# Zero matmuls ahead of the weights, the first x tile ahead of the score weights, the output weights in slot 25

## The reference, cut to what matters

```python
keys_flat = k @ Wk + bk                 # k: 32 x 512, the same for each batch
values = (keys_flat @ Wv + bv).reshape(B, S, H, D)
scores = jnp.einsum('blhe,bshe->bhls', (query @ Wq + bq).reshape(B, L, H, E), keys)
A = sparsemax(scale * scores)           # per row and head, over the 32 patterns
out = jnp.einsum('bhls,bshd->blhd', A, values)
out = jnp.transpose(out, (0, 2, 1, 3)).reshape(B, L, H * D) @ Wo + bo
x = layernorm(x + out)
s = jnp.einsum('btd,dm->btm', x, Win) + bin_
g = jnp.einsum('btmh,mh->btm', relu(s[..., None] * W1 + b1), W2) + b2
x = layernorm(x + g @ Wout + bout)
```

## Time and profile before

| | us |
|---|---|
| median of 3 runs | 1354.32 (1354.13 to 1356.15) |
| the profiled execution | 1352.76 |
| its span in the trace | 1351.0 |
| PE busy | 1251.9 (93%) |
| DVE busy | 1138.9 (84%) |
| ACT busy | 1053.6 (78%) |
| POOL busy | 703.2 (52%) |

### The profile page before, as it was taken

How to read it: one execution, slowest core, us unless ns; L and a number is a source line. 1 busy time by engine, 2 the same in 40 slices (tenths; PEclk the granted TensorE clock), 3 DMA queues, 4 the chain that set the end, 5 groups by cost and what they waited for, 6 DMA issues and landing times. The chain is left out here.

```text
span 1351.0 us, 25359 instructions
## 1 busy us (share of the span) xinstructions
PE 1251.9 (93%) x5838; PEld 867.3 (64%) x5838; DVE 1138.9 (84%) x4573; ACT 1053.6 (78%) x2269; POOL 703.2 (52%) x1674
## 2 busy tenths in 40 slices
PE   7982889999999999999999999999999999899962
PEld 6651666766776776776776776776776777555541
DVE  3977788889999999999999999999998999876764
ACT  2671756688898888899898898888899899666654
POOL 1330333345565555555556555555555556567663
PEclk9995999999999999999999999999999999999975
DMA  6380786555655655655655655655655655668733
GB/s 189 93 210 26 193 231 208 179 171 182 215 189 197 219 192 191 219 193 191 218 192 193 218 192 192 219 196 189 217 195 190 217 196 182 210 231 296 251 94 70
DMA packets 92374, 258.36 MB, mean 191 GB/s; under 512 B 16259, under 2 KB 16259, under 8 KB 75814
## 3 DMA queue, kind: packets, MB, share of 16 engines
q1 hardware_dynamic: 92198, 256.52, 58.7%
HBM read 206.13 MB, written 50.33 MB: 190 GB/s over the span
## 5 line engine op out<-in xcount | busy, mean ns | idle before, releaser
L663 PE MATMUL bank<-G_sb,pT 128*128 128x512 f32 x1024 | 461.1, 593 | 1.9 <-ACT pT L758 1.8
L663 PEld LDWEIGHTS bank<-G_sb,pT 128*128 128x128 f32 x1024 | 185.0, 191 | 185.9 <-issue 183.4
L1077 DVE MAX8 top<-bank 128x8 f32<-128x32 f32 x2048 | 212.3, 179 | 44.5 <-issue 44.5
L466 POOL TENSOR_TENSOR shift_sq<-sum,per_row_sq 128x1 f32<-128x1 f32 x256 | 96.0, 375 | 265.7 <-DVE y_sb L954 263.2
L771 ACT ACTIVATE unread<-y_sb,shift_sq 128x512 bf16<-128x512 f32 x256 | 183.9, 718 | 51.8 <-POOL minus_mean L468 51.7
L1115 DVE SCALAR_TENSOR_TENSOR acc<-hinge,w2c,acc 128x512 f32<-128x512 f32 x224 | 167.4, 748 | 61.7 <-ACT hinge L783 58.3
L783 ACT ACTIVATE hinge<-s_sb,b1c,w1c 128x512 f32<-128x512 f32 x256 | 205.8, 807 | 0.2
L588 PE MATMUL bank<-A_hi,xT_hi 128*128 128x512 f32 x512 | 204.0, 399 | 0.0
L590 PE MATMUL bank<-A_hi,xT_lo 128*128 128x512 f32 x512 | 203.9, 398 | 0.0
L589 PE MATMUL bank<-A_lo,xT_hi 128*128 128x512 f32 x512 | 203.7, 398 | 0.0
L481 POOL TENSOR_TENSOR rstd<-ve,minus_half 128x1 f32<-128x1 f32 x256 | 164.8, 644 | 43.1 <-POOL ve L476 42.8
(11 more groups left out here) (133 smaller groups left out, 2421.9 us busy)
## 6 DMA issues: line engine op xcount, KB each, us to landing
G_sb<-G_of_heads SPq DMA_DIRECT2D x128, 1024.0 KB, 5.4
x_sb<-in_L_attn_query_dram SPq DMA_DIRECT2D x128, 256.0 KB, 4.7
y_sb<-in_L_attn_query_dram SPq DMA_DIRECT2D x256, 128.0 KB, 5.4
out_dram<-o_sb SPq DMA_DIRECT2D x256, 128.0 KB, 4.7
G_of_heads<-y_sb SPq DMA_DIRECT2D x64, 256.0 KB, 3.8
y_sb<-in_L_attn_Wk_dram SPq DMA_DIRECT2D x1, 1024.0 KB, 5.7
y_sb<-in_L_attn_Wq_dram SPq DMA_DIRECT2D x1, 1024.0 KB, 8.2
y_sb<-in_L_attn_Wv_dram SPq DMA_DIRECT2D x1, 1024.0 KB
```

The costliest lines, as they stand in the source:

```text
L466: nc.gpsimd.tensor_tensor(shift_sq[:, par:par + 1], total[:, par:par + 1], per_row_sq[:], ALU.mult).then_inc(s_mean, 1)
L663: mm = nc.tensor.matmul(o_ps[i % 2][:], pT[:, bass.ds(pair_place(turn, i) + (i % H * C + c) * P, P)], G_sb[:, i % GR, c, :], start=(c == 0 ...
L1077: mx = nc.vector.max(top8[:, h, :], z_ps[i % 2][:, h * S:(h + 1) * S])
```

## The change

It does three things, and edits the waits that they need.

1. POOL fills `K_blk` (buffer `acc`) with zeros as its second fill instead of its fifth, and PE, once that fill is done, runs 7 float32 products of 128 x 128 by 128 x 256 on it into bank 7, before it waits for the keys' loads.
2. PE transposes x of tile 0 between "c" and "A" instead of after "A". ACT rounds it ahead of the first `A_hi`, DVE takes its rest ahead of the first `A_lo`. The scores of tile 0 wait for the pieces of `A_lo` one chunk at a time instead of for all four.
3. DVE splits the output weights in slot 25 (`LAG_Y`) instead of slot 1. ACT's first write to `s_sb` waits for it.

```diff
+        IDLE_PASSES = 7
...
             nc.gpsimd.memset(b2c[:], 0.0).then_inc(s_zero, 1)
+            nc.gpsimd.memset(K_blk, 0.0).then_inc(s_const, 1)
             nc.gpsimd.memset(ident[:], 0.0).then_inc(s_const, 1)
             nc.gpsimd.memset(go_on[:], 1.0).then_inc(s_const, 1)
             nc.gpsimd.memset(ones_s[:], 1.0).then_inc(s_const, 1)
-            nc.gpsimd.memset(K_blk, 0.0).then_inc(s_const, 1)
...
+            def transpose_x(turn, j):
+
+                base, i = turn * UNROLL, j - LAG_X
+                pe.wait_ge(s_x[i % XR], 16 * (turns_of(turn, j, LAG_X, XR) + 1))
+                if not isinstance(turn, int) or base + i >= 1:
+                    pe.wait_ge(s_xhi, base + i)
+                    pe.wait_ge(s_xlo, base + i)
+                for c in range(C):
+                    mm = nc.tensor.transpose(xT_ps[:, c * P:(c + 1) * P], x_sb[:, i % XR, c * P:(c + 1) * P],
+                                             ident[:])
+                mm.then_inc(s_xT, 1)
+
+            pe.wait_ge(s_const, 1)
+            for n in range(IDLE_PASSES):
+                nc.tensor.matmul(banks[7][:, 0:2 * P], acc[:, 0:P], acc[:, 0:2 * P], start=True, stop=True)
             pe.wait_ge(s_wkeys, 16 * KEY_LOADS)
             pe.wait_ge(s_const, CONSTS)
             for n, (name, c) in enumerate(STEPS):
+                if name == "A" and c == 0:
+                    pe.wait_ge(s_sev, done("keysT") + 1)
+                    transpose_x(0, 0)
...
                 for c in range(C):
+                    if first:
+                        pe.wait_ge(s_ready, c + 1)
                     nc.tensor.matmul(ps[:], hi[:, c, :], w_hi[:, c, :], start=start and c == 0, stop=False)
...
                     if base + i == 0:
-                        pe.wait_ge(s_ready, C)
                         pe.wait_ge(s_c, 2)
...
-                act.wait_ge(s_smm, n + 1)
+                if (name, c) != ("A", 0):
+                    act.wait_ge(s_smm, n + 1)
...
                 else:
+                    if c == 0:
+                        act.wait_ge(s_xT, 1)
+                        nc.scalar.copy(xT_hi[:].rearrange("p c n -> p (c n)"), xT_ps[:]).then_inc(s_xhi, 1)
+                        act.wait_ge(s_smm, n + 1)
                     nc.scalar.mul(A_hi[:, c, :], ps[:], SCALE).then_inc(s_sev, 1)
...
                     act.wait_ge(s_s, base + i + 1)
+                    if base + i == 0:
+                        act.wait_ge(s_ready, C + 2)
+                        act.wait_ge(s_c, 5)
...
+            rest_of_x(0)
             for c in range(C):
                 dve.wait_ge(s_sev, done("c") + c + 1)
...
-                if turn == 0 and j == 1:
+                if base + j == LAG_Y:
 
                     dve.wait_ge(s_wload, 16 * WLOADS)
                     nc.vector.tensor_copy(Wout_hi[:], Wout_sb).then_inc(s_ready, 1)
```

More of the change, by code:

```diff
@@ L584, in _, with three_pass @@
                 mm.then_inc(s_smm, 1)
-            def three_pass(ps, hi, lo, w_hi, w_lo, start):
+            def three_pass(ps, hi, lo, w_hi, w_lo, start, first):
                 for c in range(C):
+                    if first:
+                        pe.wait_ge(s_ready, c + 1)
                     nc.tensor.matmul(ps[:], hi[:, c, :], w_hi[:, c, :], start=start and c == 0, stop=False)
@@ L620, in slot @@
                     nc.tensor.matmul(z[:], pick_c[:], bias_rows[:], start=True, stop=False)
-                    three_pass(z, xT_hi, xT_lo, A_hi, A_lo, start=False).then_inc(s_score, 1)
+                    three_pass(z, xT_hi, xT_lo, A_hi, A_lo, start=False, first=base + i == 0).then_inc(s_score, 1)
                 lead = j - LAG_CHECK
@@ L629, in slot @@
                                      stop=True).then_inc(s_opens, 1)
[L630 to L639, removed]
+                if in_range(turn, j, LAG_X) and base + j > 0:
+                    transpose_x(turn, j)
                 if in_range(turn, j, LAG_YT):
@@ L843, in slot @@
                     nc.scalar.copy(split_of(lead)[1][0:M, :], both[0:M, :]).then_inc(s_high, 1)
-                if in_range(turn, j, LAG_X):
+                if in_range(turn, j, LAG_X) and base + j > 0:
                     i = j - LAG_X
@@ L897, in _, with rest_of_x @@
         def _(dve):
+            def rest_of_x(i):
+                dve.wait_ge(s_xhi, i + 1)
+                nc.vector.tensor_tensor(
+                    xT_lo[:].rearrange("p c n -> p (c n)"), xT_ps[:],
+                    xT_hi[:].bitcast(F32).rearrange("p c n -> p (c n)"), ALU.subtract
+                ).then_inc(s_xlo, 1)
             dve.wait_ge(s_const, CONSTS)
@@ L1036, in slot @@
                     dve.wait_ge(s_score, base + (j - LAG_SCORE) + 1)
[L1037 to L1043, removed]
-                if turn == 0 and j == 1:
+                if in_range(turn, j, LAG_X) and base + j > 0:
+                    rest_of_x(base + j - LAG_X)
+                if base + j == LAG_Y:
                     dve.wait_ge(s_wload, 16 * WLOADS)
```

## The result

| | before, us | after, us |
|---|---|---|
| median | 1353.72 (1351.49 to 1356.15, 6 runs) | 1347.19 (1346.79 to 1350.74, 6 runs) |
| the profiled execution | 1352.76 | 1350.74 |
| its span | 1351.0 | 1348.9 |

The ratio is 0.996, with a 95% interval of 0.995 to 0.997: 4 to 7 us less (the means are 5.8 us apart), where 2.8 were forecast. Two later comparisons of the same two kernels gave 0.9964 (0.9950 to 0.9978) and 0.9970 (0.9959 to 0.9980); the median over all 19 executions of the changed kernel is 1348.55. So the change is real and small, and its size is 4 to 6 us.

What follows compares the result with a forecast made beforehand. PE was taken to bound 7.83 to 23.7 us, then wait for DVE, with both nearly full from 30 to 35 us. Gains 1.1 + 1.65 + 0.1 gave 1354.3 - 2.8 = 1351.5 us, range 1347.9 to 1354.0.

Steps and rivals of the forecast that it cites:

- part 2: Tile 0's x ahead of A: first scores start at 24.1 instead of 25.77, gain 1.65 us, bounds 1.2 and 2.1.
- The sum: The gains of the three parts together: 1.1 + 1.65 + 0.1 = 2.85 us, own range 1.2 to 5.3.
- hidden under c: Before A: the transposes of tile 0's x are not hidden, so A starts and ends 0.44 us later.
- no chunk of the first scores waited for its A_lo: First scores of tile 0: chunks 0.7 us apart from 24.4; the last A_lo, done at 25.5, is wanted at 26.5.
- Part 1: Zero passes before keysT: the clock rises, then falls during keysT, which ends 1.1 us earlier, bounds 0 and 2.8.
- The rival that the clock holds: In keysT the clock stays full: 6.4 us gain with the other parts, about 1347.9 us, chance 0.15.
- Part 3: Output weights moved from slot 1 to slot 25: 2.54 us of DVE moved, gain 0.1 us, bounds 0 and 0.4.
- Slot 25 was covered: xT_lo of tile 26 slips, done at 221.2; PE wants it at 222.70, so the score product is not held.
- The sign of the rival: Slot 25 not covered: PE waits on xT_lo and the clock falls; 2.5 to 4.2 us slower, about 1357.5, chance 0.07.

Runs made afterwards that it cites:

- wout_only: The kernel before with only the output-weight split moved from slot 1 to slot 25: 1352.44 us median of 11, ratio 0.9983.
- the five or three fills and their buffer: Tiny DVE fills of an unread buffer in slot 1: five added to wout_only (1351.44 us), three to the changed kernel with 11 passes (1344.91 us).

## Why the prediction was half right

**The direction and the mechanism of part 2 were right.** The sum had 1.65 us, between 1.2 and 2.1. The trace has 1.95 from the end of c to the first scores, in every kernel with part 2, and part 2 alone a mean of 2.2 (1.4 to 2.9). The 1.74 at the scores of tile 0 look closer to 1.65 than the term was: 0.21 of a late rise of the clock hide the rest. The transposes were not hidden under c, and no chunk of the first scores waited for its A_lo. They took 0.50 us instead of 0.44, but A took 3.49 instead of 3.67, which no term had.

**Part 1: the right mechanism, a fair size.** The clock rose within the passes and fell again, 2 to 4 us after them, where the prediction had 2.9 to 4.4 from the earlier trace rows, and keysT did not hold it. In the four traces with 7 passes ahead of the old list the fall came at 8.7 to 10.5 us (predicted 9.0 to 11.5), and the passes ended at 6.6 to 7.5 (predicted 6.1 to 7.1). The term was 1.1 us between 0 and 2.8. In traces keysT won 0.0, 0.2, 0.5 and 1.4, and c ended 1.0 us sooner in the mean. By the means of the times the passes alone brought 2.0 (1.1 to 2.8), and taking them out of the whole cost some 0.6 to 2.3. If there is more than 1.1, it comes later than tile 0; the runs don't settle it. The rival that the clock holds fell. The rule of the Trainium skill that spoke for it ("TensorE: Matmul & The Clock Gate", section "Why this matters for your kernels": the clock is lost over idle gaps) is not enough here: it was lost at 10.5 us in a stretch where PE was busy in every window.

**Part 3 was the step that failed: 0.1 us in the sum, with 0.4 as its upper bound, and 1.6 (0.9 to 2.3) measured.** It has two halves. "DVE paces slots 4 to 7 by a hair, so some 0.1 us is won" was read from one window in which PE and DVE were both near full. The trace of `wout_only` has 0.66 us by tile 9. The scores of one tile followed those of the last in 5.2 to 5.7 us between tiles 3 and 8. My reading, which no run shows by itself, is that DVE leads in some of these slots and PE in others, so that taking work from DVE wins a part of it; two busy shares can't say which part. The other half, 0.8 to 1.2 us, was not in the sum at all: a loop that got shorter because five instructions ahead of it went away.

**Slot 25 was covered, but by less than I wrote.** DVE's timeline of the changed kernel from the rest of x of tile 25 to that of tile 26:

```profile
208.05 0.68 DVE L923 TENSOR_TENSOR xT_lo<-bank,xT_hi 128x512 fp32r<-128x512 f32 x1
208.65 0.98 DVE L1072 CAST Wout_hi<-s_sb 128x512 fp32r<-128x512 f32 x1
...
211.04 0.69 DVE L1079 TENSOR_TENSOR Wout_lo<-o_sb,split 1x512 fp32r<-1x512 f32 x1
211.76 1.66 DVE L1102 MAX8 top<-bank 128x8 f32<-128x32 f32 x16
...
217.06 1.19 DVE L1063 TENSOR_TENSOR u_sb<-u_raw,step 128x512 f32<-128x512 f32 x1
218.17 0.68 DVE L923 TENSOR_TENSOR xT_lo<-bank,xT_hi 128x512 fp32r<-128x512 f32 x1
```

and PE's bias product of tile 26, which needs that last row:

```profile
219.24 0.48 PE L641 MATMUL bank<-bias_rows,pick_c 128*128 128x512 f32 x1
```

With the lead of 3.46 us taken off, xT_lo slipped by 3.7 us (218.17 + 3.46 = 221.63, before 217.97) where I had 2.5. The five instructions took 3.11 us instead of 2.54, since the first took 0.98 instead of 0.42, and one that was not moved, u_sb, took 1.19. The half microsecond of u_sb need not come from the move: in the kernel before another instruction of DVE, `cum` at 220.26, took 0.97 instead of 0.42, and with the lead taken off this is where u_sb stands (217.06 + 3.46 = 220.52). The rest of x ended at 218.85, 0.4 us before PE wanted it; I had put 1.5 there. The sign of the rival was not far: with another half us it would have begun.

**The sum.** 1.65 + 1.6 + 1.1 makes 4.35, inside the 4 to 6 us of the three comparisons; with the parts as measured alone it is 2.2 + 1.6 + 2.0 = 5.8. What was missing from 2.8 is in the main part 3. That the forecast came as near as it did owes something to luck: the size of part 3 was wrong by more than its bounds, and one execution differs from the next by as much as the whole gain.

## What to carry to other kernels

Where two engines are both nearly full, don't cost the removal of work from one at nothing: follow both lists for several slots, or give it half of its time as the upper end. Before reading a small gain or loss as work, look whether loops and jumps that the edit did not touch changed their idle times; five instructions more or less ahead of them did here. And when an idle start is filled with products to raise the clock, place the fill so that it ends right where the next work begins: here 11 passes, which ended at 8.0 to 8.5 us, were worth 2.6 us, 7 passes, which ended at 6.6 to 7.5, were worth 1.0, and 15, which ended at 10.35, nothing. Last, a single trace has its own luck with the clock: compare the end of a stretch over several traces before you credit an edit with it.

## What the runs showed of the hardware that I had not expected

- A turn of the same DVE loop cost 1.22 to 1.24 or 1.49 us of idle before its first instruction, and its exit 1.14, 1.29 or 1.52, by how many DVE instructions stood ahead of it in the program; each value came back to 0.01 us in every kernel with the same number ahead.
- The trace gave a granted clock of 1.00 for keysT in the kernel before, at 214 ns a row, and 0.50 for it in the changed kernel at the same 214 ns. In these traces the granted clock in the windows says nothing until the clock has changed once; the pace of equal rows does.
- The same program ran 2 to 8 us apart from execution to execution. Where the clock fell and rose is a part of that: in the traces of the changed kernel it was at half for 10.2, 6.8 and 10.2 us of the first 20, and without passes the same preparation ended c at 19.83 to 21.10 us.
- Once the five or three fills and their buffer were in, PE's tiles followed each other in 9.166 us instead of 9.179 for 100 tiles, 1.43 us in all. The cause was not tried.
- A float32 copy of 128x512 took DVE 0.42 us in slot 1 and 0.98 in slot 25, and a subtraction 0.69 in one slot and 1.19 in another. Whether POOL, which works beside it there, causes that was not tried.
